# Codebook and ids on one partition, loaded by GpSimd; codebook scaled ahead of chunk 0

## The reference, cut to what matters

```python
cb = codebook / jnp.clip(jnp.max(jnp.abs(codebook)), 1e-08)
scale = jnp.exp(scale_log)
wg = (weight + lora_delta).reshape(O, I // GROUP, GROUP)
normalized = wg / scale
thresholds = (cb[:-1] + cb[1:]) * 0.5
idx = jnp.searchsorted(thresholds, normalized, side='left')
quantized = cb[idx]
w = jax.lax.stop_gradient(quantized - normalized) + normalized
w_q = (w * scale).reshape(O, I)
w_eff = w_q + lora_delta
return x @ w_eff.T
```

```python
a_sel = lora_a_weights[adapter_id]
b_sel = lora_b_weights[adapter_id]
scale = scaling_factors[adapter_id]
```

## Time and profile before

| | |
|---|---|
| median of 3 executions | 912.48 us |
| lowest, highest | 910.99, 912.91 us |
| profiled execution, its own time | 910.95 us |
| its span | 909.1 us |
| TensorE busy in it | 902.2 us |
| VectorE, ScalarE, GpSimd busy | 616.5, 313.2, 144.0 us |
| DMA moved | 191.51 MB, mean 211 GB/s |

### The profile page before, as it was taken

One profiled execution on the slowest core, in us unless ns is written; L12 is line 12 of the kernel. 1 busy time (PEld: TensorE's weight loads), 2 busy tenths in 40 slices (PEclk: granted clock), 3 DMA queues, 4 the chain that ended last, 5 costly groups with the idle time before them and its releaser, 6 DMA issues.

```text
span 909.1 us, 13369 instructions
## 1 busy us (share of the span) xinstructions
PE 902.2 (99%) x4670; PEld 787.0 (87%) x4670; DVE 616.5 (68%) x1312; ACT 313.2 (34%) x503; POOL 144.0 (16%) x298
## 2 busy tenths in 40 slices
PE   8999999999999999999999999999999999999998
PEld 7999998888998888888888888888888888888886
DVE  6889899865587968976456566566566566566563
ACT  5678778411324433231322222222222222222220
POOL 0100010111001001414213113113113113113110
PEclk9999999999999999999999999999999999999999
DMA  8523330765412033556887887887888887887875
GB/s 340 208 76 122 119 125 24 259 211 166 142 50 94 4 135 94 216 211 225 280 277 258 284 274 262 282 272 263 285 272 266 280 265 270 286 270 263 287 225 184
DMA packets 60540, 191.51 MB, mean 211 GB/s; under 512 B 7965, under 2 KB 10678, under 8 KB 58554
## 3 DMA queue, kind: packets, MB, share of 16 engines
q1 hardware_dynamic: 49610, 159.02, 50.5%
q0 software_dynamic: 10432, 31.35, 11.6%
q10 hardware_dynamic: 432, 0.30, 0.1%
HBM read 158.93 MB, written 32.23 MB: 210 GB/s over the span
## 4 chain that ended last, share of the span: by engine, by line
PE 95%; DMA 4%; SPq 0%; ACT 0%; DVE 0%; issue 0%
PE bank L857 28%; PE bank L519 15%; PE bank L520 15%; PE bank L521 15%; PE bank L840 5%; PE bank L831 5%; DMA t_lo<-t_scratch 3%; PE bank L665 2%; PE bank L905 2%; PE bank L931 2%; PE bank L932 2%; PE bank L933 2%; DMA m_raw<-m1t 1%; PE bank L774 1%; PE bank L580 1%; PE bank L537 0%
## 5 line engine op out<-in xcount | busy, mean ns | idle before, releaser
L857 PE MATMUL bank<-g_hi,xs 128*128 128x512 f32 x448 | 145.2, 395 | 0.0
L857 PE MATMUL bank<-t_hi,xs 128*128 128x512 f32 x336 | 113.3, 396 | 0.3 <-DMA t_lo<-t_scratch 0.2
L490 POOL DMA_DIRECT2D p1sel<-p_scratch x128 | 65.3, 510 | 278.9 <-issue 278.8
L857 PEld LDWEIGHTS bank<-g_hi,xs 128*128 128x128 f32 x448 | 83.3, 188 | 16.3
L857 PE MATMUL bank<-g_lo,xs 128*128 128x512 f32 x224 | 88.3, 394 | 0.0
L977 ACT ACTIVATE xs<-x_raw 128x1024 fp32r<-128x1024 f32 x60 | 61.9, 1056 | 76.1 <-PE bank L857 55.7
L1309 DVE TENSOR_TENSOR xs<-x_raw,xs 128x1024 fp32r<-128x1024 f32 x60 | 75.4, 1279 | 12.0 <-ACT xs L977 11.5
L519 PE MATMUL bank<-gx,xs 128*128 128x304 f32 x256 | 77.5, 303 | 0.0
L521 PE MATMUL bank<-gx,xs 128*128 128x304 f32 x256 | 77.5, 303 | 0.0
L520 PE MATMUL bank<-gx,xs 128*128 128x304 f32 x256 | 77.3, 302 | 0.0
L857 PEld LDWEIGHTS bank<-t_hi,xs 128*128 128x128 f32 x336 | 62.1, 188 | 15.2 <-DMA t_lo<-t_scratch 2.9
(11 more groups left out here) (325 smaller groups left out, 2060.9 us busy)
## 6 DMA issues: line engine op xcount, KB each, us to landing
t_hi<-t_scratch SPq DMA_DIRECT2D x82, 512.0 KB, 4.7
t_lo<-t_scratch SPq DMA_DIRECT2D x82, 512.0 KB, 6.2
x_raw<-xq SPq DMA_DIRECT2D x16, 1024.0 KB, 6.8
out<-ost SPq DMA_DIRECT2D x63, 256.0 KB, 4.3
p1sel<-p_scratch POOLq DMA_DIRECT2D x64, 192.0 KB, 4.4
w_raw<-wall SPq DMA_DIRECT2D x16, 512.0 KB, 4.4
w<-e_scratch SPq DMA_DIRECT2D x6, 1024.0 KB, 5.1
ea<-e_scratch POOLq DMA_DIRECT2D x8, 644.0 KB, 4.5
```

The source lines that it names most:

```text
L490: pool.dma_start(f(p1sel[b][STK * s:STK * s + STK, cs]), p1_dram[bass.ds(i * STK, STK), cs]).then_inc(sems[b], 16)
L857: mm = nc.tensor.matmul(bk[j][:], l[:, c, :], m[:, c, :], start=first and c + k == 0, stop=c + k == KH + 1, skip_group_check=True)
```

## The change

The codebook and the ids are loaded to one partition, by GpSimd at its very start, each as 64 values. All tiles that hold them before the broadcast by TensorE shrink to one partition. VectorE waits for the codebook before the first w_lo and does the six scaling steps and the two for the midpoints there; the rounds h = 1 and 2 follow the first w_lo, the rounds 3 to 5 stay behind w_lo of row 1. Of the scale steps, 0 to 7 stand in between, and 8 to 13 behind the low part of the LoRA operand. The first semaphore increment for TensorE's codebook steps is moved from the count's cast to the sum before it, the copy of the columns stands ahead of the LoRA's first low part, and `w_split(2)` behind the copies of the third step. TensorE's three codebook steps stand earlier in row 1: after (0,5), (0,7) and (1,2) instead of (1,0), (1,2) and (1,6). In row 0 the low pass of chunk 1 follows chunk 1 itself; chunk 2 has none behind it.

```diff
-CB_AT = {(1, 0): 0, (1, 2): 1, (1, 6): 2}
+CB_AT = {(0, 5): 0, (0, 7): 1, (1, 2): 2}
...
-        idc = small("idc", [P, T // SEQ], I32)
+        idc = small("idc", [1, T // SEQ], I32)
...
-        cb = row("cb", [P, LV])
-        tt_ = row("tt_", [P, LV + 1])
-        reach = row("reach", [P, LV])
+        cb = row("cb", [1, LV])
+        tt_ = row("tt_", [1, LV + 1])
+        reach = row("reach", [1, LV])
...
-        cbook_b = cbook.rearrange("(a n) -> a n", a=1).to_broadcast([P, LV])
-        ids_b = ids.rearrange("(a n) -> a n", a=1).to_broadcast([P, T // SEQ])
+        cbook_r = cbook.rearrange("(a n) -> a n", a=1)
+        ids_r = ids.rearrange("(a n) -> a n", a=1)
...
             load_w(2)
-            sp.dma_start(idraw[:], ids_b).then_inc(ld_ids, 16)
             load_w(3)
...
         @block.gpsimd
         def _(pool):
+            pool.dma_start(cb[:], cbook_r).then_inc(ld_cb, 16)
+            pool.dma_start(idraw[:], ids_r).then_inc(ld_ids, 16)
             pool.wait_ge(ld_ids, 16)
...
-                if c == 0:
-                    row0_low(0)
-                if c > 1:
+                if c < 2:
+                    row0_low(c)
+                elif c > 2:
                     row0_low(c - 1)
...
-            act.dma_start(cb[:], cbook_b).then_inc(ld_cb, 16)
...
-            def codebook_scale(k):
-                if k == 0:
-                    v.wait_ge(ld_cb, 16)
-                    link(nc.vector.tensor_scalar(vcomp[:], cb[:], -1.0, None, ALU.mult))
...
+            v.wait_ge(ld_cb, 16)
+            mag = vcomp[0:1, :]
+            link(nc.vector.tensor_scalar(mag, cb[:], -1.0, None, ALU.mult))
+            link(nc.vector.tensor_tensor(mag, mag, cb[:], ALU.max))
+            link(nc.vector.reduce_max(val0[0:1, :], mag, AX_X))
+            link(nc.vector.tensor_scalar(val0[0:1, :], val0[0:1, :], 1e-8, None, ALU.max))
+            link(nc.vector.reciprocal(val0[0:1, :], val0[0:1, :]))
+            link(nc.vector.tensor_scalar(cb[:], cb[:], val0[0:1, 0:1], None, ALU.mult))
+            link(nc.vector.tensor_tensor(tt_[:, 1:LV], cb[:, 0:LV - 1], cb[:, 1:LV], ALU.add))
+            link(nc.vector.tensor_scalar(tt_[:, 1:LV], tt_[:, 1:LV], 0.5, None, ALU.mult))
...
             v.wait_ge(ws_hi, 1)
             lo_of(w_lo[0][:, 0:2, :], w_raw[0][:, 0:2, :], w_hi[0][:, 0:2, :]).then_inc(ws_lo, 1)
+            for h in (1, 2):
+                midpoints(h, 0)
+                link(midpoints(h, 1))
             for c in range(KC):
                 m1_split(c)
                 if c == 1:
                     w_split(0)
-                if c > 1:
-                    codebook_scale(c - 2)
             w_split(1)
             v.wait_ge(ld_pk, 16)
-            nc.vector.tensor_tensor(tt_[:, 1:LV], cb[:, 0:LV - 1], cb[:, 1:LV], ALU.add)
             link(scale_step(0))
-            nc.vector.tensor_scalar(tt_[:, 1:LV], tt_[:, 1:LV], 0.5, None, ALU.mult)
-            link(scale_step(1))
...
+            for h in range(3, 6):
+                midpoints(h, 0)
+                link(scale_step(2 * h - 5))
+                midpoints(h, 1)
+                link(scale_step(2 * h - 4))
+            link(nc.vector.tensor_tensor(reach[:], tt_[:, 0:LV], tt_[:, 1:LV + 1], ALU.is_lt))
+            nc.vector.reduce_sum(rs2[0][0:1, 0:1], reach[:], AX_X).then_inc(cols_ok, 1)
+            link(scale_step(7))
+            nc.vector.tensor_copy(cnt[0:1, 0:1], rs2[0][0:1, 0:1])
+            v.wait_ge(cols_mm, 1)
+            nc.vector.tensor_copy(cols[:, 0:3], bk[3][0:LV, 0:3]).then_inc(cols_ok, 1)
```

More of the change, by code:

```diff
@@ L221, in build @@
         valid = row("valid", [P, LV])
-        idraw = row("idraw", [P, T // SEQ], I32)
-        idf = row("idf", [P, T // SEQ])
+        idraw = row("idraw", [1, T // SEQ], I32)
+        idf = row("idf", [1, T // SEQ])
         one1 = row("one1", [P, 1])
@@ L1350, in _, with midpoints @@
             link(nc.vector.memset(tt_[:, LV:LV + 1], 4.0))
[L1351 to L1364 removed]
+            v.wait_ge(ld_cb, 16)
[8 more added lines that the diff above has]
+            link(nc.vector.tensor_scalar(tt_[:, 1:LV], tt_[:, 1:LV], 0.5, None, ALU.mult))
+            def midpoints(h, side):
+                half = 1 << h
+                view = tt_[:, 0:LV].rearrange("p (b w) -> p b w", w=2 * half)
+                mid = view[:, :, half:half + 1].to_broadcast([1, LV // (2 * half), half - 1])
+                part = view[:, :, half + 1:2 * half] if side else view[:, :, 1:half]
+                return nc.vector.tensor_tensor(part, part, mid, ALU.max if side else ALU.min)
             v.wait_ge(ws_hi, 1)
             lo_of(w_lo[0][:, 0:2, :], w_raw[0][:, 0:2, :], w_hi[0][:, 0:2, :]).then_inc(ws_lo, 1)
+            for h in (1, 2):
+                midpoints(h, 0)
+                link(midpoints(h, 1))
             for c in range(KC):
@@ L1402, in _ @@
             nc.vector.tensor_scalar(selm[:], iota, cols[:, 3:4], cols[:, 2:3], ALU.is_equal, ALU.mult).then_inc(cols_ok, 1)
-            w_split(2)
+            v.wait_ge(la_hi_s, 2)
+            lo_of(lb_hl[64:P, :], lb_raw[64:P, :], lb_hl[64:P, :]).then_inc(la_lo_s, 1)
+            for k in range(8, 14):
+                link(scale_step(k))
             v.wait_ge(cols_mm, 3)
@@ L1407, in _ @@
             nc.vector.tensor_copy(valid[:], bk[3][:, 192:256]).then_inc(comp_ok, 1)
+            w_split(2)
             v.wait_ge(comp_ok, 1)
```

27 lines of the change are left out of this document (removed).

## The result

| | before | changed |
|---|---|---|
| median | 911.36 us (5 executions, 910.34 to 912.91) | 915.4 us (5 executions, 913.16 to 916.07) |
| profiled execution, its span | 910.95, 909.1 us | 913.16, 911.2 us |
| ratio, changed to before | | 1.004, 95% interval 1.0029 to 1.0051 |

The changed kernel is slower by 0.4%, and its median lies outside the predicted range on the side of the rival in which the codebook comes late. With two executions more, the kernel before has a median of 911.36 and not 912.48, so a forecast of 1.0 us less stands against a measured 4.0 us more.

The account below looks back on a forecast made before the run. TensorE, busy 902.2 of 909.1 us, bounds the kernel, so only idle time in front can move. Shorter paths to row 1 (0.27) plus earlier loads (0.7) give about 1.0 us: 912.48 to 911.5 us, range 910.3 to 913.0.

Parts of the forecast that it names:

- the codebook comes late: Rival: GpSimd's codebook load waits at busy DMA engines, delaying VectorE's first w_lo; 1.7 to 2.6 us slower than before; chance 0.08.
- faster .11, same .84, slower .05: Chances for the whole time: 0.84 within 0.2% (1.8 us) of before, 0.11 faster by more, 0.05 slower by more.
- The landing L: Time the codebook's GpSimd load lands, before VectorE's first w_lo: taken as 4.5 us, between 3.6 and 8.1.
- break-even of 6.4: Codebook landing time up to which VectorE's new wait costs nothing; from 6.4 on each us later costs a us.
- What L costs: VectorE's wait before the first w_lo: nothing at landing 4.5; in general chunk 3 starts at landing plus 7.4 us.
- TensorE's clock: No term in the prediction; TensorE's passes at the start were priced at 0.53 us each.
- Earlier arrivals d: Start of the load stream, without the codebook broadcast on ScalarE's queue: loads 0.7 us earlier, bounds 0.12 and 1.25.
- The first rival: The DMA dip at 5.5 to 8 us belongs to the start, not the codebook: gain 0.4 us, 912.1; chance 0.25.
- The low pass: Chunk 1's low pass on TensorE moved into the idle time before chunk 2: 0.16 us gained of its 0.53.
- The 0.27 us of VectorE's loop: Six codebook steps out of VectorE's chunk loop in row 0: w_lo of row 1 starts 0.27 us sooner.
- The codebook steps of TensorE: TensorE's codebook steps placed earlier in row 1: slack 0.6 us at the first, nothing gained, nothing lost.
- The third rival: The start gives back more than its bytes, for instance chunk 0 landing quicker: 2 us or more, 910.4; chance 0.10.

Follow-up runs that it names:

- second set: The changed kernel itself run again, unaltered, eight executions: 913.95 us against 911.5 for the kernel before, ratio 1.0027.
- e4_fill: Changed kernel plus three more matmuls on zeros in front and four after each of chunk 0's first two passes: 911.75 us against 911.44 before.
- e12_gpsimd_probe: e2_cb_on_act plus three further 256-byte GpSimd loads, one after the other, data unused; one execution: 911.73 us beside 911.18.
- e5_changed_again: The changed kernel run again, nothing altered, eight executions: 913.95 us against 911.5 for the kernel before, ratio 1.0027.
- e1_rows_only: Kernel before with only codebook and ids loaded to one partition by GpSimd, engine orders unchanged: 910.5 us against 911.44, ratio 0.9989.
- e3_low_pass_only: Kernel before with only chunk 1's low pass moved directly behind chunk 1: 911.3 us against 911.44, ratio 0.9999.
- e9_six_steps_front: Kernel e8 with the codebook loaded by ScalarE behind w_raw and six scaling steps before the first w_lo: 910.18 us against 911.1 before.
- e8: Kernel before with one-partition loads by GpSimd and chunk 1's low pass moved, codebook steps left in place: 909.89 us against 911.5, ratio 0.9988.
- e11: The same kernel as e8, run again beside others: 910.18 us against 911.1 for the kernel before, ratio 0.9986.
- e2_cb_on_act: Changed kernel with the one-partition codebook load issued by ScalarE behind w_raw instead of by GpSimd: 910.9 us against 911.44 before, ratio 0.9997.

## Why the prediction was wrong

The forecast was 911.5 us with faster .11, same .84, slower .05. Measured was 915.4, and 913.95 in the second set. The median left the range by the clock, which the sum doesn't have: e4_fill, with the late codebook and without the low clock, is at 911.75, well inside 910.3 to 913.0. The late codebook turned the forecast gain of 1.0 us into a loss of 0.7 us (spans of 909.1 and, in e4_fill, 909.8). Step by step:

**The landing L: mis-sized, and this is the step that failed first.** 4.5 was taken between 3.6 and 8.1, because the 128 KB load of ScalarE (4.9 us, L = 5.8) was "far larger". Measured was 7.1: 0.5 us of the difference is the issue (1.42 instead of 0.9), the other 2.1 us the way to the landing (5.6 instead of 3.6). Size was the wrong measure. The row nearest in time was that 128 KB load, and its 4.9 us, from an issue at 1.42, would have given 6.3, just short of the break-even of 6.4 and still 0.8 us too early. The bounds held it. The rival "the codebook comes late" had 0.08, and its mechanism, place and break-even were right; "only 16 small packets, not 128, have to land" was the argument against it, and e12_gpsimd_probe shows that few and small packets take 5 us all the same.

**What L costs: right in size, in part by luck.** By the prediction chunk 3 starts at L + 7.4, which is 14.5 with L = 7.1, and row 1 stands 8.73 us behind it: 23.2. e4_fill, which has this wait and the full clock, starts chunk 3 at 14.59 and row 1 at 23.20. But the path was another. The prediction runs it over m_lo of chunk 1 at VectorE; in e4_fill that was ready by 12.54, and its pass began at 13.02, since TensorE had to do the low pass of chunk 0 (11.32, held by m_lo of chunk 0) and two more passes first. Terms that were too long made up for it: the four midpoint steps took 0.6 us, not 0.7, and the eight steps 1.8 us, not 1.87 (the figures given for them add up to 1.8 as well). That one partition costs what 128 do was right.

**TensorE's clock: missing from the sum altogether.** Every pass behind the new wait was priced at 0.53 us. The earlier trace rows shows matmuls already at that pace, and I took it as given. It failed in two ways: in the first trace the clock was low before TensorE met the new wait and rose only at 14.5, and in e5_changed_again it had risen and fell after the waits. Its price was 1.44 us in the one and 2.1 us in the other, read against e4_fill, where VectorE does the same at the same time and only matmuls on zeros are added. For L = 7.1 the late rival's own working gives 0.7 us over the kernel before, and that is just what e4_fill's span shows (909.8 against 909.1); the changed kernel itself lost 2.1 us in the span and 2.45 and 4.0 in the medians. So the rival's mechanism, at the L that was measured, gives a third of the span's loss.

**Earlier arrivals d: mechanism right, size low.** 0.7 was taken in the middle of 0.12 and 1.25; it was 1.17, by e1_rows_only 1.19 in row 1. The question that the trace of before left open, small packets or start, is settled by e1_rows_only and e3_low_pass_only for the packets. The rule on pieces under 512 bytes (the Trainium skill, DMA: Bandwidth & Descriptors, section Specifications) pointed to this end, and the runs agree that such pieces cost rate: 410 against 216 GB/s; the read-modify-write that it gives as the reason no run shows. The first rival, 912.1, falls.

**The low pass: 0.16 predicted in TensorE's path, 0.19 measured** at chunk 3 in e3_low_pass_only, and no time, as VectorE's path holds row 1. **The 0.27 us of VectorE's loop** was hidden in the changed kernel; e9_six_steps_front, with those steps in front and the codebook in time, has row 1 0.2 to 0.3 us before e8 and e11. **The codebook steps of TensorE: nothing,** as predicted, for the wrong start of row 1 as well. The third rival, a start that gives back 2 us or more, falls: with the new loads and the clock up, row 1 is at 21.01 at the earliest, 1.5 us before 22.50.

**The account in row 1,** from 22.50: loads 1.2 us earlier (21.31), the wait 1.9 later (21.32 to 23.20), the clock 1.4 later (24.64) or 2.1 later, with another 0.2 from VectorE (25.47). Net +2.1 and +3.0, and the spans went from 909.1 to 911.2 and 911.8. Of the median's shift in the first set, 4.0 us, this explains 2.1 to 3.0; in the second set, 2.45, all of it. What made the first set's other four executions 1 to 2 us slower than any trace here stays open: they had a mean clock of 0.996, and so had six of the second set, at 913.28 to 914.56. Open too is why the clock rises at 5.87 in one execution of a kernel and at 14.5 in another (with the same waits in front of the first pass but for 0.3 us), how long a wait brings it down, and what in GpSimd's queue makes the delay.

## What to carry to other kernels

Before an engine that feeds TensorE's first passes is made to wait for a small load, take that load's landing from a row of the same stretch and the same queue, not from its size, and where there is none, time it first. Here a load of 256 bytes that is wanted early was best on ScalarE's queue right behind the first operand (e2_cb_on_act, 910.9), and worse ahead of it (912.96) or on GpSimd (913.95). Price a new gap of TensorE near its start twice: once for the gap, and once for the passes behind it at the lower clock, less the slack that follows; the second may come to nothing or to 2 us in the same kernel. And when an edit makes an operand land at another time, leave its consumer where it was (e8_rows_and_low): the gain of the loads stays, and the late landing costs nothing.

## What the runs showed of the hardware

- A broadcast of 32 KB in 256-byte pieces held the whole stream of loads back by 1.2 us, though its packets were put down at 3.9% of the engines' time; 5.5 to 8 us moved at 213 to 221 GB/s in the three traces with it and at 381 to 415 in the eleven without.
- 256 bytes through GpSimd took 4.7 to 5.8 us in every trace that has such a load, all of them within the first 24 us; on ScalarE's queue it took 3.9 to 4.3 us behind 128 KB (issued at 1.33, seen at 5.19 to 5.58 in three traces), and 1.6 us as the first of all (0.89 to 2.49).
- That first small load put off the 128 KB behind it by 1.55 us, for an issue 0.55 us later.
- A VectorE step of 1 x 64 took 0.17 to 0.25 us, hardly less than one of 128 x 64 (0.19 and 0.25).
- TensorE's grant fell back to 1.2 GHz in the start after waits of 1.27 and 1.23 us (at 9.28, until 16.11) and after one of 3.23 us (8.14 to 14.96); it stayed up through waits of 1.52 and 0.61 us (e2_cb_on_act). With eight matmuls on zeros between the first passes and three more ahead of them it stayed at 2.4 GHz with VectorE's wait as it was (matmuls 0.53 us apart by threes from 11.96 on).
